# A graph attention block and a graph message block on Trainium2: ACT makes the finishing tile's root of the variance ahead of four adjacency loads instead of behind them

## The chip, the cores and the metric

One core of a Trainium2 chip (trn2) runs the whole program. The metric is the device time of one execution in microseconds (us). Times inside the program come from one profiled execution. Engines: PE is TensorE, DVE is VectorE, ACT is ScalarE, POOL is GpSimd, SP is SyncE. ACT, SP and POOL also issue DMA transfers, each in the order of its own program.

## What is computed

Two layers over the same graph of 8192 nodes with 128 features. `adj` is an 8192 x 8192 matrix of zeros and ones in float32.

```python
h = relu(layernorm(x))
Wh = h @ W
e = leaky_relu(Wh @ a1 + (Wh @ a2).T, 0.2)
att = softmax(where(adj > 0, e, -9e15), axis=-1)
x = x + relu(att @ Wh)
h = relu(layernorm(x))
node = h @ W1
hw = einsum('nc,kcf->nkf', h, W2)
m = einsum('nk,nkf->nf', node, hw)
x = x + relu(adj @ m + node @ b)
```

`layernorm` divides by the root of the variance plus 1e-5. The change concerns that root in the second `layernorm`.

## The kernel before

Rows are worked on in 8 blocks of 1024 (`NB = 8`), columns of `adj` too, so that `adj` is 64 squares. A "turn" is two squares, a "half turn" one; a row block has four turns (`IT = 4`), thus eight half turns, and the program has 64. `p` is 0 or 1 for the half turn within its turn. Each half turn has four steps, `k` = 0 to 3.

A square of `adj` (4 MB in float32) fills two of the four quadrants of `adj_sb`, 0 and 1 for p = 0, 2 and 3 for p = 1. A quadrant comes in with eight DMAs of 256 KB: SP issues four and ACT the other four (`load_upper`, which calls `load_quadrants`, L291 to L299). ACT turns `adj` into bytes (`cast`, L525 to L532, L529: two casts per quadrant, the second of which counts up `adj_cast[q]`), DVE transposes the bytes (`turn_squares`, L933), ACT stores the result as `maskT_d` for the second layer, and DVE makes the attention weights of two tiles per step (`weigh`, L1009, written to the four buffers `p_sb[:, r]` with r = 2 (k mod 2) + b). PE multiplies these weights with the node features into `ot_ps` (L820, 16 records per tile) and counts up `p_used[r]`, for which `weigh` waits before it writes a buffer again.

From the second row block on, each half turn also finishes one tile of 128 rows of the block before, spread over the steps (`finish_tile` of every engine):

- step 0, DVE: `att` (L980).
- step 1, DVE: `att` (L985), the sum with x into `keep` (L990; it waits for `kept`, which POOL counts up once the store of the same buffer has landed), `bn_stats` (L993), `bn_aggr` to `mv` (L996, counts up `mv_done`). All of this stands between the two `weigh` of step 1. ACT: waits for `mv_done`, then the root `std` (L577, counts up `std_done`).
- step 2, DVE: waits for `std_done`, `rstd` (L999), `xn` (L1002), then the second `weigh` of the step. PE: after the first tile of the step it transposes `xn` (L796), after the second it needs `hT` for the node product (L784, waits for `h_done`) and for two head products (L789). ACT: casts part 1 of quadrant 2p (`cast_ahead`), makes `hT` (`relu_h`, L571), copies `node` and the bias, scales eight heads (L595).
- step 3: two more head products on PE, eight more scalings on ACT. When these are done POOL adds up the heads (L406, three instructions, then L409), splits the sum (L421, L423) and stores `msg_d` (L426) and `keep_d` (L431). Only then does it take up the next tile, for which it first confirms that the tile's other stores have landed (`confirm`, L396 to L400), which counts up `kept`.

ACT's own order of a half turn is `turn`, L625 to L663. Behind a step's loads stand the finishing work of the step and the casts. Step 1 of a finishing half turn reads: four loads of quadrant 3 - 2p, the root, the cast of quadrant 2p part 0; step 2 follows with the cast of part 1 and `hT`. The loads of step 1 wait for `adj_cast[3 - 2p]`, which the cast of step 0 has just counted up (L657 and L658). The quadrant that they fill is cast in step 2 of the next half turn at the earliest (L663).

At the end of a row block DVE makes the four weights of the next block's first two steps in advance (`start_weights`) and the denominators before it comes to the next `finish_tile`. In the last row block the last turn issues no loads. After the last row block, the last eight tiles are finished among the second layer's products (L679 on); these call `finish_tile` directly and have no loads.

Of the kernel before, what the change touches and what calls it, by code (L numbers as in the profile page):

```python
# [38 lines left out]
def build(nc, x, adj, W, a1, a2, W1, W2, b, out):  # L39
# [28 lines left out]
    with ctx:  # L68
# [191 lines left out]
        def ends_block(jg):  # L260
            return isinstance(jg, int) and jg == IT - 1
# [29 lines left out]
        def load_quadrants(eng, ib, jg, p, h, quadrants):  # L291
            q = 2 * p + h
            for part in range(2):
                for a in quadrants:
                    eng.dma_start(adj_sb[a * SQ:(a + 1) * SQ, q, part * T * COLS:(part + 1) * T * COLS]  # L295
                                  .rearrange("r (t n) -> r t n", n=COLS),
                                  adj_v[bass.ds(ib, 1), 2 * h + part, :, :,
                                        bass.ds((2 * jg + p) * BLK + a * COLS, COLS)]
                                  .rearrange("i r t n -> (i r) t n")).then_inc(adj_in[q], 16)  # L299
# [186 lines left out]
        def _(act):  # L486
# [32 lines left out]
            def load_upper(i, q):  # L519
                if isinstance(i, int) and i >= NB * IT:  # L520
                    return
                act.wait_ge(adj_cast[q], i)
                load_quadrants(act, i // IT, i % IT, q // 2, q % 2, (2, 3))

            def cast(q, part, count, squared_before):  # L525

                act.wait_ge(adj_in[q], 16 * 2 * A * count)
                act.wait_ge(squared, squared_before)
                ins = act.activation(m8[:, q // 2, 2 * (q % 2) + part, :],  # L529
                                     adj_sb[:, q, part * T * COLS:(part + 1) * T * COLS], ACT.Copy, scale=EDGE)  # L530
                if part == 1:
                    ins.then_inc(adj_cast[q], 1)  # L532
# [40 lines left out]
            def finish_tile(k, p, u, m, t, pb, cast_ahead=None, relu_done=False):  # L573

                if k == 1:
                    act.wait_ge(mv_done, m + 2)
                    act.activation(std[:, :], mv[:, 1:2], ACT.Sqrt, bias=eps[:, :]).then_inc(std_done, 1)  # L577
                if k == 2:
                    if cast_ahead:
                        cast_ahead()  # L580
                if k == 2:
                    if not relu_done:
                        relu_h(m)
                    act.wait_ge(node_done, m + 1)
                    act.activation(node[:, :], NODE, ACT.Copy).then_inc(node_copied, 1)  # L585
                    act.wait_ge(kept, m + 1)
                    act.activation(keep[:, p, D:2 * D], BIAS, ACT.Copy).then_inc(node_copied, 1)
                    act.wait_ge(node_copied, 2 * m + 3)
                    act.wait_ge(prod_read, m + 1)
                if k >= 2:  # L590
                    for g in ((0, 1) if k == 2 else (2, 3)):
                        act.wait_ge(hw_done, 4 * m + g + 1)
                        for j in range(4):
                            head = 4 * g + j
                            ins = act.activation(prod[:, head, :], hw_ps[g % 2][:, j * D:(j + 1) * D], ACT.Copy,  # L595
                                                 scale=node[:, head:head + 1])
                        ins.then_inc(hw_scaled[g % 2], 1)

            def load_xt(pb):
                act.wait_ge(mv_done, T * pb + 1)  # L600
                act.dma_start(xt[:, :, :], x_v[bass.ds(pb, 1)].rearrange("i p t f -> (i p) t f")).then_inc(xt_in, 16)

            def copy_sums(ib):
                if not (isinstance(ib, int) and ib == 0):
                    act.wait_ge(u_read, T * ib)
                    act.wait_ge(den_read, ib)
                for h, (t0, t1) in enumerate(GROUPS):
                    if h < 2:
                        act.wait_ge(ot_done, 2 * ib + h + 1)
                    else:  # L610
                        act.wait_ge(p_used[3], 4 * IT * (ib + 1))
                    act.activation(ut[:, t0:t1, :].rearrange("p t f -> p (t f)"),
                                   ot_ps[h][:, 0:(t1 - t0) * ROW], ACT.Copy).then_inc(ot_copied, 1)

            def convert(ii, first, t):
                s, r = t // T, t % 2
                for ib in range(2):
                    if not on_dve(first, t, ib):
                        act.wait_ge(masks_in[s % 4], 16 * (ii * (NB // 4) + s // 4 + 1))
                        if not (first and t < 2):  # L620
                            act.wait_ge(conv_used[r][ib], ii * (NT // 2) + t // 2)
                        act.activation(mask32[:, r, ib, :], masks[:, s % 4, ib, t % T // 4, :, t % 4], ACT.Copy)\  # L622
                           .then_inc(conv_act, 1)

            def turn(i, ib, jg, finish, last):  # L625
                for p in range(2):
                    n = 2 * i + p
                    for k in range(C):

                        if k == 1:  # L630
                            if isinstance(i, int) and i == 0 and p == 0:
                                load_upper(1, 2)
                            load_upper(i + 1 + p, 3 - 2 * p)
                        if k == 3:
                            load_upper(i + 2, 2 * p)
                        if k == 0:
                            act.wait_ge(squared, A * n + A)
                            act.dma_start(maskT_d[bass.ds(2 * jg + p, 1), bass.ds(ib, 1), :, :]
                                          .rearrange("s i p w -> (s i p) w"),
                                          mt[:, p, :, :].rearrange("p c n -> p (c n)")).then_inc(mt_stored[p], 16)  # L640
                        if ends_block(jg) and p == 1 and k == 2:
                            load_xt(ib)
                        if ends_block(jg) and p == 1 and k == 3:
                            if last:
                                convert(0, True, 0)
                            copy_sums(ib)
                        ahead = None if last else lambda: cast(2 * p, 1, i + 2, A * n + A)
                        if finish:
                            u = i - IT
                            finish_tile(k, p, u, 2 * u + p, 2 * jg + p, ib - 1, ahead)  # L650
                        elif k == 2 and ahead:
                            ahead()
                        if isinstance(i, int) and i == 0 and p == 0 and k == 0:
                            for part in range(2):
                                cast(3, part, 1, 0)
                        elif k == 0:
                            if not (last and p == 1):  # L657
                                cast(3 if p == 0 else 1, 1, i + 1 + p, A * n)  # L658
                        if k == 1 and not last:
                            cast(2 * p, 0, i + 2, A * n + A)  # L660
                        sums_wait = not finish and ends_block(jg) and p == 1
                        if k == (3 if sums_wait else 2) and not last:
                            cast(2 * p + 1, 0, i + 2, A * n + A)  # L663

            attention_loop(act, turn, loads=True)

            def take_bank(ii, ib):
# [11 lines left out]
            for t in range(NT):  # L679
                mi, at = t // PERIOD, t % PERIOD  # L680
                if mi < T:
                    m = (NB - 1) * T + mi
                    u, p = (NB - 1) * IT + mi // 2, mi % 2
# [463 lines left out]
```

## Time and profile before

| | us |
|---|---|
| runs of the kernel | 1750.59, 1784.58, 1797.03 (median 1784.58) |
| the profiled execution's own time | 1749.66 |
| its span in the trace | 1747.9 |
| around the span (launch and end) | 1.76 |
| PE busy in the span | 1701.2 (97%) |
| DVE busy | 1290.1 (74%) |
| ACT busy | 1089.2 (62%) |
| POOL busy | 548.7 (31%) |

The granted TensorE clock averages 0.994 of its upper level over the span. The profiled execution is one of the quicker ones: the median of the three runs stands 34.9 us above it. Times of single instructions are read from the profiled execution; "start, us" in its rows counts from the span's start. ACTq is ACT's own instruction queue, which issues DMAs; an engine's idle time stands in brackets at a row's end, with what ended it.

### The profile page before, as it was taken

To read this page: it belongs to the slowest core of one execution; us is meant where nothing else is said; L and a number is where in the kernel's file an instruction comes from. 1 tells how busy PE (TensorE), PEld (TensorE's weight loads), DVE (VectorE), ACT (ScalarE), POOL (GpSimd) and SP (SyncE) were. 2 spreads that over 40 slices of the span, in tenths; PEclk is the share of its full clock that TensorE was granted. 3 is DMA by queue.
4 is the path that set the end of the run, shared out by engine and by line. 5 is a ranking of instruction groups with operands and counts; after the bars stand their busy time and mean duration, and the time that the engine had idled before them with its cause. 6 is when DMAs were issued, how large, how long until landed. Compare 5 with 4: busy or idle time off the path is not lost.

```text
span 1747.9 us, 35898 instructions
## 1 busy us (share of the span) xinstructions
PE 1701.2 (97%) x11311; PEld 1468.8 (84%) x11311; DVE 1290.1 (74%) x1775; ACT 1089.2 (62%) x1889; POOL 548.7 (31%) x522
## 2 busy tenths in 40 slices
PE   8889899999999999999999999999999999999998
PEld 5789788888888988988888888898777788888886
DVE  8679688888888898888888888888566443533534
ACT  5554466767666677676676767663655655555554
POOL 0000044454453544544445445355444200000000
PEclk9999999999999999999999999999999999999999
DMA  9999999999999999999999999987533345453430
GB/s 236 280 347 367 324 279 315 298 328 303 292 321 310 300 315 307 306 303 313 311 295 312 320 291 315 311 245 288 208 140 145 122 171 193 154 204 144 168 144 24
DMA packets 316753, 452.23 MB, mean 259 GB/s; under 512 B 21072, under 2 KB 291616, under 8 KB 298912
## 3 DMA queue, kind: packets, MB, share of 16 engines
q1 hardware_dynamic: 164928, 228.63, 44.2%
q10 hardware_dynamic: 144944, 203.58, 39.0%
q0 software_dynamic: 6832, 19.41, 3.4%
q8 instruction: 26, 0.43, 0.1%
q14 instruction: 23, 0.19, 0.0%
HBM read 364.46 MB, written 87.07 MB: 258 GB/s over the span
## 4 chain that ended last, share of the span: by engine, by line
PE 81%; DMA 5%; SPq 4%; DVE 3%; issue 2%; ACTq 2%; ACT 1%; POOL 1%; DVEq 0%; POOLq 0%
PE ot_ps L820 42%; PE ot_ps L877 13%; PE mt_ps L877 13%; PE hw_ps L789 12%; SPq L295 3%; DMA maskT_d<-mt 2%; ACTq L295 2%; DMA xt<-in_x_dram 1%; ACT wh_mask L529 1%; DMA adj_sb<-in_adj_dram 1%; PE h_ps L784 1%; SPq L310 1%; DVE att L985 1%; DVE p_sb L1009 1%; POOL prod L406 1%
## 5 line engine op out<-in xcount | busy, mean ns | idle before, releaser
L820 PEld LDWEIGHTS ot_ps<-wh_mask,p_sb 128*128 128x128 f32 x8192 | 945.7, 193 | 84.6 <-issue 69.8
L820 PE MATMUL ot_ps<-wh_mask,p_sb 128*128 (+1 forms) x8192 | 954.7, 277 | 25.6 <-DVE p_sb L1009 20.7
L1009 DVE SCALAR_TENSOR_TENSOR p_sb<-zb,qcol,mt 128x1024 f32<-128x1024 uint8 (+1 forms) x512 | 729.7, 1442 | 17.9 <-DVE mt L933 10.0
L529 ACT ACTIVATE wh_mask<-adj_sb 128x2048 uint8<-128x2048 f32 x256 | 485.2, 1921 | 70.3 <-issue 53.4
L406 POOL TENSOR_TENSOR prod<-prod 128x1024 f32<-128x1024 f32 (+2 forms) x192 | 333.8, 1739 | 567.8 <-ACT prod L595 550.6
L1057 DVE CAST mask<-adj_sb 128x1024 fp32r<-128x1024 uint8 x272 | 204.0, 757 | 244.9 <-PE mt_ps L877 243.2
L622 ACT ACTIVATE mask<-adj_sb 128x1024 fp32r<-128x1024 uint8 x240 | 255.2, 1064 | 173.8 <-PE ot_ps L877 173.6
L595 ACT ACTIVATE prod<-hw_ps,node 128x128 f32<-128x128 f32 x1024 | 278.7, 383 | 113.2 <-PE hw_ps L789 111.7
L877 PE MATMUL mt_ps<-mask,msgs 128*128 128x512 f32 x1024 | 282.6, 398 | 2.1 <-DVE mask L1057 1.1
L877 PE MATMUL ot_ps<-mask,msgs 128*128 128x512 f32 x1024 | 274.7, 390 | 1.1 <-DVE mask L1057 0.5
L789 PE MATMUL hw_ps<-wcat,hT 128*128 128x512 f32 x512 | 240.7, 592 | 0.0
L877 PEld LDWEIGHTS mt_ps<-mask,msgs 128*128 128x128 f32 x1024 | 191.0, 188 | 51.4 <-issue 13.4
L877 PEld LDWEIGHTS ot_ps<-mask,msgs 128*128 128x128 f32 x1024 | 191.6, 188 | 43.8 <-issue 3.8
L933 DVE STREAM_TRANSPOSE mt<-wh_mask 128x512 f32<-128x512 f32 x256 | 179.8, 703 | 25.4 <-ACT wh_mask L529 14.2
L789 PEld LDWEIGHTS hw_ps<-wcat,hT 128*128 128x128 f32 x512 | 88.6, 190 | 61.8 <-issue 61.2
L577 ACT ACTIVATE std<-mv,eps 128x1 f32<-128x1 f32 x64 | 19.3, 302 | 184.5 <-issue 156.9
L999 DVE RECIPROCAL rstd<-std 128x1 f32<-128x1 f32 x64 | 10.4, 162 | 91.7 <-ACT std L577 91.7
L421 POOL CAST msg<-msg 128x128 fp32r<-128x128 f32 x56 | 67.6, 1208 | 9.4 <-POOL msg L409 9.4
L434 POOL DMA_DIRECT2D zb<-zrow_d x7 | 3.8, 544 | 180.7 <-DVE p_sb L1009 115.5
L426 POOL DMA_DIRECT2D msg_d<-msg x56 | 31.6, 564 | 43.3 <-POOL msg L423 39.6
L585 ACT ACTIVATE node<-h_ps 128x16 f32<-128x16 f32 x64 | 11.8, 184 | 52.5 <-PE h_ps L784 52.5
L990 DVE TENSOR_TENSOR keep<-att,xt 128x128 f32<-128x128 f32 x64 | 23.3, 364 | 28.6 <-POOLq L400 9.7
(108 smaller groups left out, 575.4 us busy)
## 6 DMA issues: line engine op xcount, KB each, us to landing
adj_sb<-in_adj_dram SPq DMA_DIRECT2D x536, 256.0 KB, 7.7
adj_sb<-in_adj_dram ACTq DMA_DIRECT2D x488, 256.0 KB, 8.9
maskT_d<-mt ACTq DMA_DIRECT2D x64, 1024.0 KB, 10.3
adj_sb<-maskT_d SPq DMA_DIRECT2D x32, 2048.0 KB, 7.7
keep_d<-keep POOLq DMA_DIRECT2D x64, 128.0 KB, 6.0
p_sb<-keep_d SPq DMA_DIRECT2D x4, 2048.0 KB, 12.0
msg_d<-msg POOLq DMA_DIRECT2D x56, 128.0 KB, 5.8
msgs<-msg_d SPq DMA_DIRECT2D x7, 1024.0 KB, 9.0
```

The costliest lines, as they stand in the source:

```text
L295: eng.dma_start(adj_sb[a * SQ:(a + 1) * SQ, q, part * T * COLS:(part + 1) * T * COLS] .rearrange("r (t n) -> r t n", n=COLS), adj_v[bass.d ...
L406: pool.tensor_tensor(prod[:, 0:n, :], prod[:, 0:n, :], prod[:, n:2 * n, :], ALU.add)\
L421: pool.tensor_copy(high, msg32[:, :]).then_inc(cut_step, 1)
L529: ins = act.activation(m8[:, q // 2, 2 * (q % 2) + part, :], adj_sb[:, q, part * T * COLS:(part + 1) * T * COLS], ACT.Copy, scale=EDGE)
L595: ins = act.activation(prod[:, head, :], hw_ps[g % 2][:, j * D:(j + 1) * D], ACT.Copy, scale=node[:, head:head + 1])
L622: act.activation(mask32[:, r, ib, :], masks[:, s % 4, ib, t % T // 4, :, t % 4], ACT.Copy)\
L789: pe.matmul(hw_ps[g % 2][:, :], hT[:, :], wcat[:, g * HB:(g + 1) * HB], start=True, stop=True)\
L820: ins = pe.matmul(ot_ps[h][:, (t - t0) * ROW:(t - t0 + 1) * ROW], p_sb[:, r, t * P:(t + 1) * P], rows, start=begin and t == t0, stop=end a ...
L877: ins = pe.matmul(acc_ps[2 * ib + h][:, :], msgs[:, ORDER[s] * T + t % T, c, :], mask32[:, r, ib, h * HB:(h + 1) * HB], start=t == 0 and c ...
L933: dve.transpose(mt_squares[:, p, c, :, :, :], m8_squares[:, p, c, :, :, :]).then_inc(squared, 1)
L1009: dve.scalar_tensor_tensor(p_sb[:, r, :], zbf[:, bass.ds((ib % 2) * BLK, BLK)], qcol[:, bass.ds(tile + b_, 1)], mtb[:, p, k // 2, :, 2 * ( ...
L1057: dve.tensor_copy(mask32[:, r, ib, :], masks[:, s % 4, ib, t % T // 4, :, t % 4])\
```

## The change

The block of ACT's step 1 that issues the loads moves from ahead of `finish_tile` to behind it. The first `cast` of step 1 stays behind both. In half turns that finish no tile (the first row block), the order is what it was. No instruction is added or removed, and no other engine's program changes.

```diff
                     for k in range(C):
 
-                        if k == 1:
-                            if isinstance(i, int) and i == 0 and p == 0:
-                                load_upper(1, 2)
-                            load_upper(i + 1 + p, 3 - 2 * p)
                         if k == 3:
                             load_upper(i + 2, 2 * p)
...
                         elif k == 0:
                             if not (last and p == 1):
                                 cast(3 if p == 0 else 1, 1, i + 1 + p, A * n)
+                        if k == 1:
+                            if isinstance(i, int) and i == 0 and p == 0:
+                                load_upper(1, 2)
+                            load_upper(i + 1 + p, 3 - 2 * p)
                         if k == 1 and not last:
                             cast(2 * p, 0, i + 2, A * n + A)
```

On ACT, at step 1 of the first half turn of a finishing row block (p = 0), before. The first cast is that of step 0; the ISA rows are waits and set-up of addresses, and the one of L576 is the wait for `mv_done`:

```order
L529 ACTIVATE wh_mask<-adj_sb 128x2048
L295 ISA x2
L295 DMA adj_sb<-in_adj_dram 32x8x256
L295 ISA
L295 DMA adj_sb<-in_adj_dram 32x8x256
L295 ISA
L295 DMA adj_sb<-in_adj_dram 32x8x256
L295 ISA
L295 DMA adj_sb<-in_adj_dram 32x8x256
L576 ISA
L577 ACTIVATE std<-mv,eps 128x1
```

The same place now:

```order
L529 ACTIVATE wh_mask<-adj_sb 128x2048
L576 ISA
L577 ACTIVATE std<-mv,eps 128x1
L295 ISA x2
L295 DMA adj_sb<-in_adj_dram 32x8x256
L295 ISA
L295 DMA adj_sb<-in_adj_dram 32x8x256
L295 ISA
L295 DMA adj_sb<-in_adj_dram 32x8x256
L295 ISA
L295 DMA adj_sb<-in_adj_dram 32x8x256
```

The root and its wait have moved past the four loads.

On ACT, from step 0 to step 1 of the second half turn (p = 1) of the same turn, before (the first row is the store of the transposed mask):

```order
L638 DMA maskT_d<-mt 128x4096
L529 ACTIVATE wh_mask<-adj_sb 128x2048
L295 ISA
L295 DMA adj_sb<-in_adj_dram 32x8x256
L295 ISA
L295 DMA adj_sb<-in_adj_dram 32x8x256
L295 ISA
L295 DMA adj_sb<-in_adj_dram 32x8x256
L295 ISA
L295 DMA adj_sb<-in_adj_dram 32x8x256
L576 REGISTER_ALU
L577 ACTIVATE std<-mv,eps 128x1
```

The same place now:

```order
L634 DMA maskT_d<-mt 128x4096
L529 ACTIVATE wh_mask<-adj_sb 128x2048
L576 REGISTER_ALU
L577 ACTIVATE std<-mv,eps 128x1
L295 ISA
L295 DMA adj_sb<-in_adj_dram 32x8x256
L295 ISA
L295 DMA adj_sb<-in_adj_dram 32x8x256
L295 ISA
L295 DMA adj_sb<-in_adj_dram 32x8x256
L295 ISA
L295 DMA adj_sb<-in_adj_dram 32x8x256
```

Again the root passes the four loads. Whatever waits behind `mv_done` on ACT's queue now includes them, while before it was only the root and the casts.

## Rows read from the trace of the kernel before

**Rows 1.** Waits by engine: for whom; us in total, times, longest.

```profile
DVE rstd L999 <- ACT std L577: 91.7, 53, 2.5
...
ACT std L577 <- DVE mv L996: 27.6, 7, 6.8
```

**Rows 2.** Busy time in one stretch: length, PE, PEld, DVE, ACT, POOL, PEclk, DMA, GB/s.

```profile
494.00:641.00 147.00, 146.30 (x1119) 130.31 (x1119) 128.24 (x157) 100.95 (x199) 67.85 (x65) 1.00 1.09 308
```

**Rows 3.** Timeline of PE, node product of five half turns: start us, us, engine, line.

```profile
212.68 0.41 PE L784 MATMUL h_ps<-wcat,hT 128*128 128x144 f32 x2
...
486.56 0.41 PE L784 MATMUL h_ps<-wcat,hT 128*128 128x144 f32 x2
...
505.61 0.41 PE L784 MATMUL h_ps<-wcat,hT 128*128 128x144 f32 x2
...
1163.70 0.41 PE L784 MATMUL h_ps<-wcat,hT 128*128 128x144 f32 x2
...
1181.78 0.41 PE L784 MATMUL h_ps<-wcat,hT 128*128 128x144 f32 x2
```

**Rows 4.** Timeline of all engines, one half turn inside a row block, 713 to 725.

```profile
713.39 0.29 DVE L990 TENSOR_TENSOR keep<-att,xt 128x128 f32<-128x128 f32 x1
...
713.94 9.10 PE L820 MATMUL ot_ps<-wh_mask,p_sb 128*128 x80
...
714.17 0.18 DVE L996 BATCH_NORM_AGGREGATE mv<-stat 128x2 f32<-128x6 f32 x1 [0.15 <-DVE stat L993]
714.31 1.28 DVE L1009 SCALAR_TENSOR_TENSOR p_sb<-zb,qcol,mt 128x1024 f32<-128x1024 uint8 x1
...
715.45 1.91 ACT L529 ACTIVATE wh_mask<-adj_sb 128x2048 uint8<-128x2048 f32 x1
...
715.61 5.38 POOL L406 TENSOR_TENSOR prod<-prod 128x1024 f32<-128x1024 f32 x3 [8.31 <-ACT prod L595]
716.14 2.92 DVE L1009 SCALAR_TENSOR_TENSOR p_sb<-zb,qcol,mt 128x1024 f32<-128x1024 uint8 x1
717.80 2.89 ACTq L295 DMA_DIRECT2D adj_sb<-in_adj_dram  x4
720.82 0.29 ACT L577 ACTIVATE std<-mv,eps 128x1 f32<-128x1 f32 x1 [3.46 <-issue]
...
721.15 0.16 DVE L999 RECIPROCAL rstd<-std 128x1 f32<-128x1 f32 x1 [2.09 <-ACT std L577]
...
724.62 0.26 ACT L571 ACTIVATE hT<-h_ps 128x128 f32<-128x128 f32 x1
724.93 0.51 PE L784 MATMUL h_ps<-wcat,hT 128*128 128x144 f32 x2
724.94 0.54 POOL L431 DMA_DIRECT2D keep_d<-keep  x1
```

**Rows 5.** Timeline of ACT and DVE at the first half turn of a row block.

```profile
497.80 2.89 ACTq L295 DMA_DIRECT2D adj_sb<-in_adj_dram  x4
...
499.82 0.18 DVE L996 BATCH_NORM_AGGREGATE mv<-stat 128x2 f32<-128x6 f32 x1 [0.15 <-DVE stat L993]
...
504.62 0.26 ACT L571 ACTIVATE hT<-h_ps 128x128 f32<-128x128 f32 x1
```

**Rows 6.** The same at the first finishing half turn of the program.

```profile
199.40 6.25 ACTq L295 DMA_DIRECT2D adj_sb<-in_adj_dram  x4
...
205.25 0.18 DVE L996 BATCH_NORM_AGGREGATE mv<-stat 128x2 f32<-128x6 f32 x1 [0.16 <-DVE stat L993]
```

**Rows 7.** Timeline of POOL and DVE, a half turn of the last row block without loads.

```profile
1172.63 6.45 POOL L406 TENSOR_TENSOR prod<-prod 128x1024 f32<-128x1024 f32 x3 [7.34 <-ACT prod L595]
...
1176.18 1.11 DVE L1002 TENSOR_SCALAR xn<-keep,mv,rstd 128x128 f32<-128x128 f32 x1
...
1183.79 0.54 POOL L431 DMA_DIRECT2D keep_d<-keep  x1
```

**Rows 8.** DMA issues of the page: times, KB each, median us from issue to landing.

```profile
keep_d<-keep POOLq DMA_DIRECT2D x64, 128.0 KB, 6.0
```

## Prediction

> **What bounds the kernel now.** I read the waits of each engine first, then the busy time by stretches, then the timeline of one half turn inside a row block and of one at a block's start. The waits show what the change aims at: DVE stood idle 91.7 us in 53 places until ACT had made the root, while ACT itself seldom waited for `mv`, 27.6 us in 7 places [rows 1]. But the stretches say that this idle time is not what ends last: in a whole row block PE is busy 146.30 of 147.00 us, DVE 128.24, ACT 100.95 [rows 2]. So the gain is not the idle time of DVE but what of it reaches PE.
>
> How much reaches PE is read from the node product L784, which comes once per half turn. From 212.68 to 1163.70 there are 52 half turns, and the next one, at 1181.78, comes 18.08 us later in a half turn in which PE waits for nothing [rows 3]. 52 x 18.08 = 940.16, and 1163.70 - 212.68 = 951.02: PE loses 10.86 us to all waits in this stretch. A block's first half turn takes 505.61 - 486.56 = 19.05, thus 0.97 over [rows 3]. There are six block starts in the stretch; the last one shows no such excess, so 5 x 0.97 = 4.85 stays there and **6.0 us** lie inside the blocks. Those are the small waits in which `xn`, the `weigh` behind it or `hT` come a tenth or two late.
>
> **The change part by part.** No operation goes or comes. What moves is the root: it passes four loads, and the four loads now stand behind ACT's wait for `mv_done`.
>
> *Inside a block, ACT.* `mv` ends at 714.17 + 0.18 = 714.35, the cast of step 0 at 715.45 + 1.91 = 717.36, the loads start at 717.80 and the root at 720.82 [rows 4]. In the new order the root finds its `mv` 3.0 us old, runs right behind the cast at about 717.3, and is over before the loads start, for these still wait for that cast. Root 3.4 us earlier, loads at the same time. The root's own 0.29 us leaves the path loads, casts, `hT`; `hT` ends at 724.62 + 0.26 = 724.88 and PE takes it at 724.93 [rows 4], so this path had no slack, and now has 0.2. The DMA issue of the four loads costs ACT's queue the same 2.89 us as before.
>
> *Inside a block, DVE.* Its 2.09 us of idle time before `rstd` [rows 4] goes: `rstd` follows the `weigh` that ends at 716.14 + 2.92 = 719.06. With that the 6.0 us of PE can go: **-6.0** at best, since the second `weigh` of step 2 has 2 us more.
>
> *At a block's start.* Here `mv` is late, because DVE comes from the weights made in advance and from the denominators: it ends at 499.82 + 0.18 = 500.00, while the loads had started at 497.80 [rows 5]. The loads now wait for it. From the start of the loads to the end of `hT` is 504.62 + 0.26 - 497.80 = 7.08 [rows 5], of which 0.20 was the root's turn on ACT (the next cast starts 0.2 behind the root), so 6.88. With loads at 500.00 + 0.25 (two waits and the set-up of an address, estimated from the 0.44 between the cast's end at 717.36 and the loads at 717.80, which holds the same steps) `hT` ends at 507.13 and PE has it at 507.18; before, PE took it at 505.61 [rows 3]. **1.57 us** per block start. Could DVE's new slack pull `mv` forward? The fourth weight made in advance needs a buffer which PE frees only at the end of step 3, and DVE was at that limit already, so I take nothing. Five such starts make 7.9; at the sixth, in the last row block, `mv` is less late, and I take 1.3: together **+9.1**. Bounds per start: 1.3 (loads at once behind `mv`) and 2.1 (0.6 + another issue wait), so 8 to 12.
>
> *The first finishing half turn.* `mv` ends at 205.43, the loads had taken 6.25 from 199.40, and PE took `hT` at 212.68 [rows 3, 6]. By the same sum `hT` ends at 205.43 + 0.25 + 6.88 = 212.56: **0**. If the four loads again take 6.25 instead of 2.89, +3.3; I take the 2.89 of rows 4 and 5, for the queue has had six more microseconds to drain.
>
> *The loads' data.* The quadrant filled is cast in step 2 of the next half turn, over 20 us after the loads' start inside a block. At the late block starts 2.5 us of this are lost. Cost nothing; were that cover gone, each us would be one of PE.
>
> *DVE against POOL.* This is the cost that the trace of before does not show in place. In rows 4 the `weigh` that starts 0.5 us into POOL's sum takes 2.92 instead of 1.28: one of the two stands still while the other works. Today DVE's idle 2.09 us leave POOL alone for the rest of its sum, which takes 5.38, and `keep_d` is stored at 724.94, 9.33 us after the sum's start. The half turn at 1172 has no loads, so its root is early, as all will be now: `xn` takes 1.11, POOL's sum 6.45, and the store comes 1183.79 - 1172.63 = 11.16 after its start [rows 7]. So the store moves by 1.8 us. It lands 6.0 us after its issue [rows 8]: before, at 724.94 + 6.0 = 730.9, and DVE writes the same buffer of `keep` one half turn after 713.39, at 731.6. It had 0.6 us of slack; now `keep` waits until about 732.8, 1.2 late. `mv` is then 1.2 late too, which ACT doesn't feel (3.0 us old). But the second `weigh` of step 1, 0.92 behind `keep` [rows 4], now starts at 733.7, and POOL's next sum at 715.61 + 18.2 = 733.8. If DVE is first, nothing is lost. If POOL is, this `weigh` stands still for the sum's first instruction (in rows 4 from 715.61 to 719.06 - 1.28 = 717.78, some 2.2 us), the next `weigh` falls into its second one, and the first tile of step 2, which PE wants four tiles behind its 713.94 (1.8 us each, 721.1 in rows 4), comes about 0.4 late, the second 0.2 more: about 0.6 per half turn. Bounds: 0 and 0.65 over 46 half turns inside blocks, 0 to +30. The two starts are within 0.1 us of one another, and each loss of PE shifts them apart again, so I take a third: 0.2 x 46 = **+9**.
>
> The Trainium skill, page "SBUF — State Buffer", section "Who interferes with whom", says that DVE and GpSimd hold a shared pair of ports as an exclusive lock for a whole instruction, and the other blocks fully. The 2.92 of rows 4 agrees. By that rule only the order counts, and no bandwidth is lost; a half turn in which DVE always goes first would cost nothing, one in which POOL does costs the stand-still above, so the rule speaks for both ends of the bound and not for the middle.
>
> **Sum.** -6.0 + 9.1 + 0 + 9 = +12.1 us, on the profiled execution's 1749.66: 1761.8, +0.7%. The median of the runs shown stands 34.9 above that execution, from 1784.58; the same sum on it gives **1796.7**, and that is my forecast for the time of the changed kernel. The runs shown spread over 2.6% for reasons that the trace does not hold, which is why the range is wider than the cases.
>
> **The rivals.**
>
> *Only the gain.* The root is early, `mv` at the block starts comes 2 us earlier since DVE has slack, and the store of `keep` lands in time. For it: DVE loses 91.7 us of idle time. Against it: PE frees the buffers no earlier. -6: 1743.7, or 1778.6 on the median.
>
> *Loads that wait for `mv` in every half turn (slower).* If the later store of `keep` and the standing still of DVE add up, `mv` comes behind the cast of step 0, and the loads, casts and `hT` slide with it. Place: step 1 of each half turn inside a block. It decides once `mv` is over 3.0 us later than in rows 4; I expect 1.2. From there each us costs PE one, and with 0.65 for the two `weigh` per half turn, 46 x 0.65 + 9 - 6 = +33 already stands before the first load is late; 0.2 us of lateness over 46 makes +42: 1791.7, or 1826.6 on the median. For it: the store's landing and the buffer form a loop from tile to tile. Against it: in the trace only block ends show a slow landing.
>
> *Nothing to see.* The port costs nothing and block starts eat the gain: +3.1, 1752.8 or 1787.7 on the median.
>
> **How the numbers follow.** Forecast 0.5, nothing to see 0.25, only the gain 0.12, loads late 0.13. A measurement of this kernel can tell about 2% (35 us) from no change. All but the slower rival lie within it; its 0.13 and a little of the forecast's upper end give slower 0.13, and a gain of 2% would need more than all the 10.86 us that PE waits, so faster 0.03, left for what I have not seen; same 0.84. Range: from the gain on a quick execution, 1749, to 1818, the median with the lower end of the slower rival.
>
> **What would show it.** Right: `rstd` no longer waits for the root; ACT waits for `mv` at seven places only, before loads; L784 to L784 near 20.6 at block starts; `keep` waits for POOL's confirmation inside blocks; `keep_d` stored over 10.5 us behind the sum's start. Wrong: block starts of 19 us (then `mv` moved), 18.08 throughout with no wait before `keep` (the port costs nothing), or waits of ACT for `mv` in most half turns (the slower rival).

## The result, and the profile after

The changed kernel took 1791.02 us in the median of four runs (1781.36 to 1800.29); the kernel before, run beside it, 1769.55 (1750.59, 1754.51, 1784.58, 1797.03). The ratio is **1.022**, with a 95% interval of 1.012 to 1.032; it compares only runs that lie within 1.5% of their kernel's quickest, which leaves out the last two of before, and the plain medians give 1.012. A second measurement on another occasion (r1_again below) gave 1.024 (1.008 to 1.041). By the ratio the change makes the kernel slower by about 2%; that it is slower is clear, whether by more or less than 2% isn't.

Execution against execution: 1786.58 us for the profiled one of after (span 1784.8) against 1749.66 (span 1747.9), **36.9 us** more, where the sum had +12.1.

The waits of after that answer to [rows 1], with two of PE:

```profile
DVE keep L990 <- POOLq L400: 107.3, 47, 7.3
DVE keep L990 <- DMA xt<-in_x_dram: 20.0, 6, 6.5
...
DVE rstd L999 <- ACT std L577: 4.3, 6, 0.8
```

```profile
ACT std L577 <- DVE mv L996: 27.7, 10, 5.9
```

```profile
PE ot_ps L820 <- DVE p_sb L1009: 30.5, 59, 3.5
PE h_ps L784 <- ACT hT L571: 11.1, 7, 2.2
```

The change did what it says: DVE's 91.7 us of waiting for the root are 4.3. But 107.3 us of another wait have come, in 47 places, for POOL's confirmation that the buffer of `keep` is free. It is larger than the one removed. Both lie off PE for the most part; on PE, waits for weights add up to 30.5 us in 59 places, against 20.7 us in 13 before.

Busy time of one stretch, 200 to 1200 us, of after (columns as in [rows 2]):

```profile
200.00:1200.00 1000.00, 970.64 (x7302) 857.29 (x7302) 847.99 (x1018) 657.75 (x1274) 535.98 (x421) 1.00 1.09 297
```

and of the kernel before:

```profile
200.00:1200.00 1000.00, 992.83 (x7576) 884.73 (x7575) 869.18 (x1056) 676.90 (x1316) 461.87 (x435) 1.00 1.07 302
```

PE was busy 992.83 of 1000 us and is 970.64 now, at the same granted clock. POOL is busier, 535.98 against 461.87, though it got through fewer instructions (421 against 435): it stands still within them.

Where the 36.9 us lie, by the node product L784 as in [rows 3]:

```profile
212.50 0.51 PE L784 MATMUL h_ps<-wcat,hT 128*128 128x144 f32 x2
...
855.22 0.41 PE L784 MATMUL h_ps<-wcat,hT 128*128 128x144 f32 x2
...
873.74 0.41 PE L784 MATMUL h_ps<-wcat,hT 128*128 128x144 f32 x2
...
1198.21 0.41 PE L784 MATMUL h_ps<-wcat,hT 128*128 128x144 f32 x2
...
1234.37 0.41 PE L784 MATMUL h_ps<-wcat,hT 128*128 128x144 f32 x2
...
1258.90 0.41 PE L784 MATMUL h_ps<-wcat,hT 128*128 128x144 f32 x2
```

The same 52 half turns take 1198.21 - 212.50 = 985.71 us, 34.7 more than the 951.02 of before. The six half turns at block starts take 127.46 together against 113.31: +14.2. The other 46 take 858.25 against 837.71: +20.5; in the middle of a block one takes 18.52 (873.74 - 855.22), where PE's work is 18.08. Another 2.4 come at the last block's end (24.53 between the last two rows against 22.08 before).

One half turn inside a block, timeline of after:

```profile
856.68 0.54 POOL L431 DMA_DIRECT2D keep_d<-keep  x1
...
861.72 0.28 DVE L985 TENSOR_SCALAR att<-att,rden 128x128 f32<-128x128 f32 x1
...
863.96 0.29 DVE L990 TENSOR_TENSOR keep<-att,xt 128x128 f32<-128x128 f32 x1 [1.96 <-POOLq L400]
864.14 6.26 POOL L406 TENSOR_TENSOR prod<-prod 128x1024 f32<-128x1024 f32 x3 [6.92 <-ACT prod L595]
...
864.73 0.18 DVE L996 BATCH_NORM_AGGREGATE mv<-stat 128x2 f32<-128x6 f32 x1 [0.15 <-DVE stat L993]
864.87 2.72 DVE L1009 SCALAR_TENSOR_TENSOR p_sb<-zb,qcol,mt 128x1024 f32<-128x1024 uint8 x1
...
865.62 0.34 ACT L577 ACTIVATE std<-mv,eps 128x1 f32<-128x1 f32 x1
865.94 3.00 ACTq L295 DMA_DIRECT2D adj_sb<-in_adj_dram  x4
...
868.14 1.67 DVE L1009 SCALAR_TENSOR_TENSOR p_sb<-zb,qcol,mt 128x1024 f32<-128x1024 uint8 x1
869.96 2.05 PE L820 MATMUL ot_ps<-wh_mask,p_sb 128*128 x16 [0.17 <-DVE p_sb L1009]
...
872.53 1.31 POOL L423 TENSOR_TENSOR msg<-msg 128x128 fp32r<-128x128 f32 x1
...
874.26 0.27 ACT L587 ACTIVATE keep<-h_ps 128x128 f32<-128x128 f32 x1
874.57 0.56 POOL L426 DMA_DIRECT2D msg_d<-msg  x1 [0.73 <-ACT keep L587]
...
875.26 0.54 POOL L431 DMA_DIRECT2D keep_d<-keep  x1
```

Read against [rows 4]: the root comes right behind the cast, ahead of the loads, as foreseen. The store of `keep_d` leaves 11.12 us after the sum's start (875.26 - 864.14) instead of 9.33. DVE was ready to write `keep` at 862.0 and starts at 863.96, when the store of 856.68 has landed. The second `weigh` of step 1 then starts at 864.87, 0.7 us *behind* POOL's sum, and takes 2.72 us; before it started at 714.31, 1.3 us ahead of the sum, and took 1.28. The next `weigh` ends at 869.81, and PE, idle for 0.17 us by then, starts at 869.96.

The chain of waits of after over two such half turns (854 to 892):

```profile
by line: DMA keep_d<-keep 36.9%; PE ot_ps L820 22.8%; issue 18.4%; DVE p_sb L1009 9.0%; DVE mt L933 3.7%; DVE stat L993 1.6%; DVE keep L990 1.6%; ACT keep L587 1.5%; PE h_ps L784 1.4%; PE h_ps L796 0.6%; DVE mv L996 0.5%; POOL msg_d L426 0.
...
856.68 7.00 DMA keep_d<-keep
...
863.96 0.30 DVE keep L990
...
867.51 0.70 DVE mt L933
868.21 1.61 DVE p_sb L1009
...
869.96 2.05 PE ot_ps L820 x16
...
875.26 7.04 DMA keep_d<-keep
```

Before, the chain in this part was PE throughout. Now the landing of a 128 KB store, which DVE needs only to get its buffer back, stands in it once per half turn. One step of this view has to be read with care: it leads from PE's node product over ACT's copy L587 to the next store. That copy (874.26) belongs to the next tile; POOL's `msg_d` starts 0.73 us after POOL's own L423 ended (872.53 + 1.31 = 873.84), and in the kernel before the same 0.73 us stand there, put down to L423. So the store follows POOL's sum, and the loop takes two half turns: from the node product (855.22) 8.92 us to the start of its tile's sum, 11.12 to the store; and from a store (856.68) over its landing, `keep` and the two `weigh` 17.06 to a node product (873.74). Together that is 37.1 us, or 18.55 for one half turn, where 18.52 was measured. By the same rows a landing of 6.0 us instead of 7.0 would make it 18.05, just under the 18.08 of PE's work (an estimate): each microsecond in the loop costs half a microsecond per half turn, once the slack is gone.

A block's start, timeline of after, answering to [rows 5]:

```profile
657.55 1.75 DVE L990 TENSOR_TENSOR keep<-att,xt 128x128 f32<-128x128 f32 x1 [2.34 <-DMA xt<-in_x_dram]
...
660.00 0.29 ACT L577 ACTIVATE std<-mv,eps 128x1 f32<-128x1 f32 x1 [3.21 <-DVE mv L996]
660.41 2.90 ACTq L295 DMA_DIRECT2D adj_sb<-in_adj_dram  x4
...
661.78 2.05 PE L820 MATMUL ot_ps<-wh_mask,p_sb 128*128 128x129 f32 x16 [1.22 <-DVE p_sb L1009]
...
667.11 0.26 ACT L571 ACTIVATE hT<-h_ps 128x128 f32<-128x128 f32 x1
667.41 0.51 PE L784 MATMUL h_ps<-wcat,hT 128*128 128x144 f32 x2 [1.68 <-ACT hT L571]
```

ACT waits for `mv` with the four loads behind it, and PE waits 1.68 us for `hT`.

### The profile page after: what moved, and what is told of

It reads as the page before. It is cut to its first block, busy times and chain, and to the rows that moved or that the text cites. A ratio compares the mean times of both kernels' runs of the same rounds, so it can differ in the third digit from the quotient of the medians.

```text
span 1784.8 us, 35898 instructions
## 1 busy us (share of the span) xinstructions
PE 1714.9 (96%) x11311; PEld 1472.9 (83%) x11311; DVE 1301.6 (73%) x1775; ACT 1090.7 (61%) x1889; POOL 642.1 (36%) x522
## 4 chain that ended last, share of the span: by engine, by line
PE 42%; DMA 22%; issue 9%; DVE 8%; SPq 6%; POOL 5%; ACT 4%; ACTq 4%; POOLq 0%; DVEq 0%
DMA keep_d<-keep 15%; PE ot_ps L877 13%; PE mt_ps L877 13%; PE ot_ps L820 11%; DMA xt<-in_x_dram 6%; SPq L295 5%; DVE p_sb L1009 4%; PE hw_ps L789 4%; POOL prod L406 3%; ACTq L295 3%; ACT wh_mask L529 2%; DVE mt L933 1%; ACT prod L595 1%; DVE keep L990 1%; PE h_ps L784 1%
## 5 line engine op out<-in xcount | busy, mean ns | idle before, releaser
L820 PE MATMUL ot_ps<-wh_mask,p_sb 128*128 (+1 forms) x8192 | 965.9, 277 | 35.6 <-DVE p_sb L1009 30.5
L1009 DVE SCALAR_TENSOR_TENSOR p_sb<-zb,qcol,mt 128x1024 f32<-128x1024 uint8 (+1 forms) x512 | 748.1, 1478 | 26.4 <-PE ot_ps L820 11.2
L406 POOL TENSOR_TENSOR prod<-prod 128x1024 f32<-128x1024 f32 (+2 forms) x192 | 381.7, 1988 | 510.7 <-ACT prod L595 377.8
L595 ACT ACTIVATE prod<-hw_ps,node 128x128 f32<-128x128 f32 x1024 | 278.1, 382 | 114.2 <-PE hw_ps L789 112.8
L933 DVE STREAM_TRANSPOSE mt<-wh_mask 128x512 f32<-128x512 f32 x256 | 179.4, 701 | 22.7 <-DMA maskT_d<-mt 12.1
L990 DVE TENSOR_TENSOR keep<-att,xt 128x128 f32<-128x128 f32 x64 | 22.8, 357 | 132.8 <-POOLq L400 107.3
L409 POOL TENSOR_TENSOR msg<-prod 128x128 f32<-128x128 f32 x64 | 90.2, 1409 | 5.0
L423 POOL TENSOR_TENSOR msg<-msg 128x128 fp32r<-128x128 f32 x56 | 64.9, 1159 | 4.5
L1002 DVE TENSOR_SCALAR xn<-keep,mv,rstd 128x128 f32<-128x128 f32 x64 | 47.9, 749 | 2.3
## 6 DMA issues: line engine op xcount, KB each, us to landing
maskT_d<-mt ACTq DMA_DIRECT2D x64, 1024.0 KB, 11.1
```

Source lines behind the costliest of these rows:

```text
L406: pool.tensor_tensor(prod[:, 0:n, :], prod[:, 0:n, :], prod[:, n:2 * n, :], ALU.add)\
L409: pool.tensor_tensor(msg32[:, :], prod[:, 0, :], prod[:, 1, :], ALU.add).then_inc(prod_read, 1)
L820: ins = pe.matmul(ot_ps[h][:, (t - t0) * ROW:(t - t0 + 1) * ROW], p_sb[:, r, t * P:(t + 1) * P], rows, start=begin and t == t0, stop=end a ...
L933: dve.transpose(mt_squares[:, p, c, :, :, :], m8_squares[:, p, c, :, :, :]).then_inc(squared, 1)
L1009: dve.scalar_tensor_tensor(p_sb[:, r, :], zbf[:, bass.ds((ib % 2) * BLK, BLK)], qcol[:, bass.ds(tile + b_, 1)], mtb[:, p, k // 2, :, 2 * ( ...
```

## The experiments

Theory A: the early root lets DVE run into POOL's sum; the store goes out and lands later, DVE's write of `keep` waits for it, the weights come late; block starts are a separate and smaller price. ("The port" below is short for DVE and POOL making one another stand still.) Theory B, the rival: loads that stand behind the wait for `mv` are what costs. The table has what all kernels gave; the half turns are taken between the node products of each profiled execution, "starts" the six at block starts in sum, "inside" the other 46.

| kernel | ratio to before (95%) | starts, us | inside, mean | inside, median | inside, over 18.4 |
|---|---|---|---|---|---|
| before | 1 | 113.3 | 18.21 | 18.24 | 1 |
| after | 1.022 (1.012 to 1.032) | 127.5 | 18.66 | 18.52 | 41 |
| r1_again | 1.024 (1.008 to 1.041) | 130.0 | 18.63 | 18.63 | 40 |
| r2_start_loads_first | 1.034 (1.027 to 1.041) | 146.0 | 18.72 | 18.51 | 40 |
| r3_start_root_first | 1.024 (1.018 to 1.031) | 143.2 | 18.39 | 18.15 | 8 |
| r4_dve_held | 1.018 (1.009 to 1.026) | 134.4 | 18.83 | 18.50 | 33 |
| r5_no_root_wait | 1.018 (1.013 to 1.024) | 120.7 | 18.79 | 18.72 | 42 |
| r6_keep4 | 1.014 (1.010 to 1.018) | 142.8 | 18.32 | 18.08 | 7 |
| r7_keep4_start | 1.017 (1.014 to 1.020) | 148.2 | 18.23 | 18.08 | 6 |
| r8_before_keep4 | 1.018 (1.014 to 1.022) | 151.2 | 18.21 | 18.14 | 5 |
| r9_copy | 1.004 (0.998 to 1.009) | 125.8 | 18.22 | 18.17 | 3 |
| r10_copy_p1 | 1.004 (0.997 to 1.012) | - | - | - | - |
| r11_before_copy | 1.003 (0.998 to 1.008) | 114.2 | 18.38 | 18.40 | 12 |
| r12_before_peeled | 1.022 (1.017 to 1.027) | 154.0 | 18.25 | 18.15 | 6 |

### r1_again: the changed kernel once more

No edit.

> The changed kernel again, on the same chip as the next three. Theory A (the early root lets DVE run into POOL's sum; the store of keep_d goes out 1.8 us later and lands a microsecond slower, DVE's write of keep waits for it, and the weights of step 2 reach PE late) and theory B (the four loads behind the wait for mv are what costs, by late loads, late casts and late hT) both expect what was seen: ratio near 1.02, 18.5 us per half turn inside a block, 21.3 to 21.7 at a block's start.

Measured: 1789.22 us against 1775.41, ratio 1.024; `keep` waited 109.4 us in 46 places. The finding repeats; it tells the theories apart in nothing.

### r2_start_loads_first and r3_start_root_first: where root or loads stand first

```diff
+                        if k == 1 and (FIRST):
+                            load_upper(i + 1 + p, 3 - 2 * p)
...
-                        if k == 1:
+                        if k == 1 and not (FIRST):
                             load_upper(i + 1 + p, 3 - 2 * p)
...
-                if alone or not finish:
+                if alone or peel or not finish:
                     turn(ib * IT, ib, 0, finish, False)
```

The first line stands ahead of `finish_tile`, the second behind it; FIRST is "first half turn of a row block" in r2 and "any other" in r3. The last line writes ACT's first turn of a block out ahead of the loop.

> Root first everywhere but in the first half turn of each row block, where the loads stand first again (ACT's loop is peeled there). Theory A: the starts fall back by the 14 us that they gained, inside the blocks 18.5 us stay, so +20 to +23 us over before, ratio 1.012. Theory B: mv is late for the loads only at the starts, so nearly all goes: ratio 1.00 to 1.003, 18.2 inside the blocks.

> The opposite: root first only in the first half turn of each row block, loads first elsewhere (the same peeling). Theory A: +9 to +14 us, starts of 20.6 to 21.5 us, 18.2 inside the blocks, ratio 1.005 to 1.008. Theory B: most of the 37 us, ratio 1.015 to 1.02.

Inside the blocks the result is A's in both: 18.51 in the median where the root is first (r2), 18.15 where the loads are first (r3), though it is r2 in which the loads don't wait for the late `mv` of the block starts; inside its blocks the root waited for `mv` in six places, 0.2 to 1.0 us each. B, which expected 18.2 inside for r2, falls with this. The starts and the ratios are neither's: 24.4 to 26.1 us in five of the six starts of both kernels, so that neither is faster than the change itself. The reason is the peeling; r12_before_peeled prices it. How the starts' price splits can't be read from these two.

### r4_dve_held: ACT in the new order, DVE held back

```diff
                             load_upper(i + 1 + p, 3 - 2 * p)
+                        if k == 1 and finish:
+                            act.sem_inc(loads_gone, 1)
...
                     dve.wait_ge(std_done, m + 1)
+                    dve.wait_ge(loads_gone, m + 1)
```

> ACT's order as in the changed kernel (root, then loads), but DVE takes up the root only once ACT has issued the four loads, as late as before the change (ACT counts up a semaphore behind the loads). Theory A: inside the blocks the time falls back to about 18.2 us per half turn, keep waits no more, POOL's sum takes 5.4 us again; only the starts cost, ratio 1.005 to 1.008. Theory B: no difference from the changed kernel, ratio 1.02, 18.5 inside the blocks.

Ratio 1.018 with a median of 18.50 inside: these numbers are the ones expected by B. But of the 46 half turns only 33 are over 18.4 us, the others, in stretches, mostly at 18.2 to 18.4, near what A expected. In 25 of the 33 `keep` had waited for POOL just before; the other 8 (18.6 to 23.6 us) have no such wait, and what made them long stays open. A timeline from a slow stretch says why:

```profile
572.35 0.29 DVE L994 TENSOR_TENSOR keep<-att,xt 128x128 f32<-128x128 f32 x1 [1.98 <-POOLq L401]
...
573.25 2.70 DVE L1014 SCALAR_TENSOR_TENSOR p_sb<-zb,qcol,mt 128x1024 f32<-128x1024 uint8 x1
...
576.50 1.67 DVE L1014 SCALAR_TENSOR_TENSOR p_sb<-zb,qcol,mt 128x1024 f32<-128x1024 uint8 x1
578.09 0.15 DVE L1004 RECIPROCAL rstd<-std 128x1 f32<-128x1 f32 x1
```

The hold does nothing here: the four loads, issued from 574.69 on, are out by 577.6, and DVE arrives at 578.09, because it is late already. A late `keep` makes DVE late, DVE then works beside POOL's sum without a pause, the store is late, and the next `keep` too. A hold that comes only as late as the loads' issue doesn't get the loop out of this. At a block's start it gets out by itself: there `keep` waits for `xt` and not for POOL, and then up to six tiles, mostly three, pass until the wait for POOL is back. As a test of A against B the kernel is inconclusive; it added this.

### r5_no_root_wait: DVE early, ACT's order untouched

```diff
-                    dve.wait_ge(std_done, m + 1)
-                    dve.reciprocal(rstd[:, :], std[:, :])
+                    dve.reciprocal(rstd[:, :], ones[:, 0:1])
```

> The kernel before with ACT's order untouched; DVE's reciprocal of step 2 reads a constant one in place of the root and doesn't wait for it, so that the normalisation of the finished tiles leaves the root of the variance out. Theory A: DVE is early as in the changed kernel, so inside the blocks 18.4 to 18.6 us per half turn, keep waits for POOL in over 40 places, and the starts stay at 19: +15 to +22 us, ratio near 1.01. Theory B: ACT's order is what costs, so 1.00 or a little under (PE's 6 us of small waits gone).

Ratio 1.018, 18.72 inside. Its timeline has the pattern of after, while ACT works as before:

```profile
563.56 0.29 DVE L990 TENSOR_TENSOR keep<-att,xt 128x128 f32<-128x128 f32 x1 [2.01 <-POOLq L400]
563.68 6.28 POOL L406 TENSOR_TENSOR prod<-prod 128x1024 f32<-128x1024 f32 x3 [6.91 <-ACT prod L595]
564.48 2.68 DVE L1008 SCALAR_TENSOR_TENSOR p_sb<-zb,qcol,mt 128x1024 f32<-128x1024 uint8 x1
...
565.49 2.99 ACTq L295 DMA_DIRECT2D adj_sb<-in_adj_dram  x4
...
567.71 1.67 DVE L1008 SCALAR_TENSOR_TENSOR p_sb<-zb,qcol,mt 128x1024 f32<-128x1024 uint8 x1
568.60 0.29 ACT L577 ACTIVATE std<-mv,eps 128x1 f32<-128x1 f32 x1 [3.27 <-issue]
```

The loads go out before the root, nobody's load waits for `mv`, and the loss inside the blocks is there. This settles A against B: a DVE that is early is enough. The starts take 120.7, 7 over before, so that half of what after loses at its starts comes with the early DVE as well.

### r6_keep4, r7_keep4_start, r8_before_keep4: four buffers of keep

```diff
-        keep = sb("keep", [P, 2, 2 * D])
+        keep = sb("keep", [P, 4, 2 * D])
...
-            pool.sem_inc(kept, 1)
+            pool.sem_inc(kept, 1 + 4 - 2)
...
-                x1 = keep[:, p, 0:D]
+                x1 = keep[:, t % 4, 0:D]
```

Every other use of `keep` and of `kept` in the same way; the turns of a block are written out on DVE and ACT, and POOL's finishing as well. r6 has the order of the change, r7 that of r2, r8 that of before.

> The changed kernel with four buffers of keep instead of two (the loops over turns of DVE, ACT and POOL's finishing are written out so that the buffer's number is known). Theory A with the wait as the cause: keep waits no more for its buffer, 18.1 us per half turn inside the blocks although POOL's sum still takes over 6 us; the starts still cost, so +3 to +10 us over before, ratio 1.002 to 1.006. If the standing still at the port were the cause by itself: 18.4 to 18.6 inside the blocks and ratio 1.015 or more.

> Four buffers of keep, root first inside the blocks, loads first at each block's start: the gain of the change without either of its two prices. Theory A: 18.1 us per half turn, starts of 19: -4 to -8 us against before, ratio 0.995 to 0.998. If the port is a cause by itself: +10 or more.

> Control: the kernel before with four buffers of keep and the same loops written out. In it keep never waited for its buffer inside the blocks, so 18.2 us per half turn and ratio 1.000, within 0.2%, by either theory.

Inside the blocks A holds in the median: 18.08 in r6 and r7, PE's bare work, and 18.14 in the control; `keep` waits for POOL nowhere inside. The means are 18.32, 18.23 and 18.21, since r6 and r7 have 7 and 6 half turns over 18.4; in six of r6's seven PE waited for `hT`. POOL stands still as long as ever; its line on r6's page:

```profile
L410 POOL TENSOR_TENSOR prod<-prod 128x1024 f32<-128x1024 f32 (+2 forms) x192 | 399.6, 2081 | 516.8 <-DMA keep_d<-keep 316.6
```

A sum takes 3 x 2.08 = 6.2 us, and in the usual half turn PE loses nothing by it. So standing still at the port is not a price by itself; it is one through the buffer that comes back late. One limit of this: in r6 and r7 the second `weigh` of step 1 is always ahead of POOL's sum (1.25 us each time), so no run shows what that `weigh` behind the sum would cost with `keep` in time. The ratios (1.014, 1.017) miss what was expected, and so does the control (1.018): with the written-out turns five of the six starts take 24 to 28 us. That r6 is faster than its control (1.014 and 1.018, with intervals that overlap) is not shown.

### r9_copy, r11_before_copy: the wait moved, all loops as they are

```diff
-                x1 = keep[:, p, 0:D]
+                x1 = x1t[:, :]
...
-                    dve.wait_ge(kept, m + 1)
                     dve.tensor_tensor(x1, att[:, :], xt[:, bass.ds(t, 1), :].rearrange("p t f -> p (t f)"), ALU.add)\
...
                     dve.tensor_scalar(xn[:, :], x1, mv[:, 0:1], rstd[:, :], ALU.subtract, ALU.mult)\
                        .then_inc(xn_done, 1)
+                    dve.wait_ge(kept, m + 1)
+                    dve.tensor_copy(keep[:, p, 0:D], x1).then_inc(x1_kept, 1)
```

POOL waits for `x1_kept` before it stores. r9 has the order of the change, r11 that of before.

> The changed kernel with all its loops as they are; DVE writes the tile's sum into a buffer of its own at step 1 and copies it into keep at step 2, behind xn, and only the copy waits for the store of two tiles before. Theory A: mv no longer depends on a landing, so 18.1 us per half turn inside the blocks with POOL's sum still over 6 us; starts 20.6 to 21.5: +2 to +10 us over before, ratio 1.001 to 1.006. If standing still at the port were enough by itself: 18.4 to 18.6 and ratio 1.015 or more.

> Control: the kernel before with the copy. By either theory 18.1 to 18.3 us per half turn, starts at 19, ratio 1.000 within 0.3%.

r9 came out as A had it: 1.0035 (0.998 to 1.009), 18.17 inside; the loss inside the blocks is gone, 46 half turns take 837.97 us against 837.71 before, with the changed order and no other loop. What stays is the starts, +12.5. POOL's sum was expected over 6 us and took 5.4, with the store 10.06 us behind the sum's start, so r9 alone would not part the port from the buffer; r6 does. The control stands at 1.0025 with 18.40 inside, 0.2 over before: with a late root the copy sits just ahead of the second `weigh` of step 2, which may be the reason; this wasn't tested. It is more than the 18.3 expected.

### r10_copy_p1: root first in second half turns only

The edit of r9, with r2's two lines and FIRST = "p == 0", without peeling.

> The same copy, and root first only in the second half turn of each turn (p = 1), so that at a block's start (p = 0) the loads stand first as before. Theory A: 18.1 in second half turns, 18.1 to 18.25 in first ones, starts at 19: -2 to -6 us against before, ratio 0.997 to 0.999; it would be the first version not slower than before. Otherwise over 1.005.

Ratio 1.0044 (0.997 to 1.012), median 1763.96 against 1751.66. The interval holds the expected gain as well as a loss; no gain is shown. Its profiled execution took 1787.37, 23 us over the kernel's own median, so its half turns are not set beside the others. What made it long can be read from it, and it isn't the loop: inside the blocks neither DVE nor POOL waits for a landed store of `keep`, POOL's three instructions take 5.37, and yet a half turn inside takes 18.52 in the median. What differs is ACT's issue of the four loads:

```profile
902.26 4.58 ACTq L297 DMA_DIRECT2D adj_sb<-in_adj_dram  x4
```

It takes over 3.2 us in 19 of 48 places, in after in one of 48, and PE waits 18.5 us in 16 places for the `hT` behind it. So after's 18.5 are not of this kind. No version beat the kernel before.

### r12_before_peeled: what peeling costs

Only the peeling of r2 and r3, on the kernel before.

> Control for the two kernels whose ACT loop was peeled: the kernel before with the same peeling and nothing else. If the instructions of the peeled turn have to be fetched at each block's start, the starts take 24 to 26 us instead of 19 and the inside of the blocks 18.2: ratio 1.015 to 1.022. If peeling is free and root and loads made those starts long: ratio 1.000, starts at 19.

Ratio 1.022, inside 18.15, starts 26.3 to 27.8 (five of the six), more than expected. On ACT at a start:

```profile
655.36 2.17 ACT L595 ACTIVATE prod<-hw_ps,node 128x128 f32<-128x128 f32 x8
663.90 0.37 ACTq L638 DMA_DIRECT2D maskT_d<-mt  x1
664.44 1.91 ACT L529 ACTIVATE wh_mask<-adj_sb 128x2048 uint8<-128x2048 f32 x1 [6.90 <-issue]
```

on PE a few microseconds later, and the busy times of that stretch (columns as in [rows 2]):

```profile
671.79 3.81 PE L820 MATMUL ot_ps<-wh_mask,p_sb 128*128 128x129 f32 x16 [0.64 <-DVE p_sb L1009]
```

```profile
668.70:675.60 6.90, 4.28 (x18) 3.99 (x19) 5.43 (x8) 4.06 (x4) 0.00 (x0) 0.51 1.01 271
```

and among the DMA queues of its page, where the kernel before has 23 packets on this one:

```profile
q14 instruction: 50, 0.41, 0.1%
```

ACT stands 6.4 us with nothing that the profile shows to wait for, at the place where its program leaves the loop for code it last ran a block ago, and 27 more packets of instructions come in, two of them between 650 and 672, where the kernel before has none. That the engine stands for these packets is inferred from their coming together.

A second price follows the first. PE stood idle for 4.63 us (until 670.68), and from 668.7 to 675.6 its granted clock is 0.51, the lower level: a tile of 16 records takes 3.81 us instead of 2.05. In the kernel before the clock at this start is 1.00 (652 to 671), and in after too (655 to 672). So a part of each peeled start, at least 1.8 us for this one tile, is clock. The starts of r2, r3 and r6 to r8 are of the same length (24 to 28 us), and in their traces the clock falls to its lower level for 3.4 to 10.2 us at five of them (r6: four); their ratios are read only against kernels of the same shape.

## Why the prediction was right or wrong

The stated range, 1749 to 1818, held the time (1791.02), and the forecast of 1796.7 lies near it. But that is partly the moving reference: the median of before came out at 1769.55 with a fourth run. As a difference the forecast was +12 us or 0.7% and the measured one is 37 us or 2.2%, three times as much; that the range held is in part its width. Its lower end, 1749, is called "the gain on a quick execution", which by the sum is 1743.7; 1749 is before's own. Point by point:

- *Inside, ACT.* Right: the root runs behind the cast and is over before the loads start (865.62 and 865.94), the loads start as early as before.
- *Inside, DVE's gain of 6.0.* Right as a quantity that can be had: r6 runs at 18.08 in 32 of the 46 half turns. In after it isn't seen, for the loop takes more.
- *Block starts, +9.1.* Right in what it priced: PE's waits for `hT` are 11.1 us in 7 places; one of 2.2 us belongs to a slow DMA issue at the end of a block, 8.9 to the starts. Not in the sum was the rest of the 14.2, some 5 us. At the same starts PE waited for weights and DVE for `xt` (five places, 13.5 of its 20.0 us; before, it waited for `xt` only at the first finishing half turn), and at the last one PE ran 3.4 us (1102.6 to 1106.0) at a granted clock of 0.50, right behind its 2.2 us wait. Its step "could DVE's slack pull `mv` forward? I take nothing" was right that nothing is won; that the early DVE would make starts longer, as r5 shows by 7 us, was missed.
- *First finishing half turn, 0.* Right: 212.50 against 212.68.
- *Loads' data, 0.* Right: ACT waited for loads 10.7 us in 5 places against 8.4 in 2.
- *DVE against POOL, +9.* **This is the term that was mis-sized**: 20.5 us more inside plus the 6.0 of gain that didn't show make 26.5, or 0.58 per half turn, near the upper bound of 0.65 that the text gave. The mechanism was as told, link by link: store 11.12 us behind the sum's start (11.16 foreseen), `keep` waiting, the `weigh` of step 1 behind POOL. The step that failed is "it lands 6.0 us after its issue". It lands 7.0 us after it now. With 6.0 the `weigh` and the sum would have met within 0.1 us by the prediction's sum (by after's own rows the `weigh` would be 0.3 ahead), and I took a third of the bound; with 7.0 the sum is first by 0.7 us nearly every time, in 40 half turns of 46.
- *The rivals.* "Loads that wait for `mv`" had +33 from this very collision and is nearest in size, but its own mechanism didn't decide: inside a block `mv` ends at 864.91 and the cast at 865.78, so the loads wait for the cast as ever (ACT waited for `mv` in only two places inside the 46, 0.15 and 0.74 us), and r5 shows the loss without it. "Only the gain" and "nothing to see" fall. The chance of 0.13 for slower by over 2% was too small: all that pushed `keep` later pushed the same way, and the text treated a near tie as if it were noise about zero.
- *What would show it.* Of the five signs named for "right" three are there: `rstd` no longer waits for the root, `keep` waits for POOL inside the blocks, and `keep_d` is stored 11.1 us behind the sum's start. Two are so only roughly: starts were to take 20.6 and take 19.8 to 21.9, and ACT waits for `mv` in ten places, where seven were named.

Left open: why the store lands slower when it leaves later (next section but one), and how the starts' 14 us divide in after itself.

## What to carry to other kernels

An engine's idle time can be what keeps a neighbour's buffer cycle in time: before removing it, follow the buffer that the engine writes next back to the store that frees it, and count the slack in that loop (here 0.6 us), with the store's landing taken at its worst. Where two instructions that block one another would start within a tenth of each other, price the bad order in full. And test such a loop with one more buffer or a private copy, without peeling loops, for in this kernel the written-out turns of r12 alone cost 2%. Where a view of the chain names a releaser from another tile, check it against the same place in the kernel before.

## What the runs showed of the hardware

- The same 128 KB store landed 6.0 to 6.1 us after its issue (median of all 64) in the kernels with a late root inside the blocks (before, r3, r8, r11, r12), and 6.6 to 7.4 in those where DVE is early (after 7.0, r1 7.1, r2 6.9, r5 7.2, r6 7.2, r7 7.4, r9 6.6). Before, it leaves with the node product (724.94 and 724.93); in after, r1, r2 and r5 1.5 us behind it (875.26 and 873.74), in r9 0.9 and in r6 and r7 4.2 us in the median. So it is later, but the landing hardly grows with the delay. Which transfer it meets wasn't tried.
- DVE and POOL: a `weigh` that starts behind POOL's first sum takes 2.5 to 3.2 us in after (2.72 in the rows above) instead of 1.28, POOL's three sums 6.2 instead of 5.4. The Trainium skill, page "SBUF — State Buffer", section "Who interferes with whom", calls this an exclusive lock that the first to issue holds. The rows agree; r6 adds that the time so lost need not reach the end.
- In one execution of r4 the same code ran stretches of about 18.2 us per half turn, without the wait before `keep`, and others of 18.5, with it.
- A turn written out ahead of ACT's loop made five of six starts 7.3 to 8.8 us longer (r12), with 50 packets of instructions instead of 23. Part of it is that TensorE's granted clock fell to 0.51 for 6.9 us behind an idle time of 4.63 us.
